# Two table scatters of a slot taken apart in GpSimd's order, in a fused perceiver kernel

## The reference, cut to what matters

```python
x = x + _L0_xattn_ref(_layernorm(x), ctx_1024, ...)
x = x + _L0_attn_ref(_layernorm(x), ...)
x = x + _L0_ffn_ref(_layernorm(x), w1, w2)          # quantised weights and activations
x = x + _L1_xattn_ref(_layernorm(x), ctx_1024, ...)  # 16 heads
x = x + _L1_attn_ref(_layernorm(x), ...)             # window of 5
x = x + _L1_ffn_ref(_layernorm(x), router_w, w1, w2)

# in _L1_ffn_ref
top_v, top_i = jax.lax.top_k(softmax(x_flat @ router_w.T), 2)
for k in range(2):
    pos = ...        # place of the row in its expert's list
    slot = jnp.where(pos < C, eid * C + pos, E * C)
    buf = zeros.at[slot].add(x_flat * keep)
    out = out + expert(buf)[slot] * gate * keep
```

## Time and profile before

| what | value |
| --- | --- |
| median of 3 runs | 1499.72 us (1499.08 to 2269.69) |
| profiled execution | 1499.72 us, span 1497.9 us |
| TensorE | busy 1395.7 us, 93% |
| weight loads | 1188.2 us, 79% |
| VectorE | 886.7 us, 59% |
| ScalarE | 826.6 us, 55% |
| GpSimd | 639.2 us, 43% |

### The profile page before, as it was taken

The page is one execution under the profiler, slowest core; times in us unless marked ns, Lnnn a source line. Parts: engine busy times, 40 slices in busy tenths (PEclk is TensorE's granted clock), DMA queues, the critical chain, the costliest instruction groups (busy, mean ns, idle before and its releaser), DMA issues. The chain is left out here.

```text
span 1497.9 us, 51669 instructions
## 1 busy us (share of the span) xinstructions
PE 1395.7 (93%) x19618; PEld 1188.2 (79%) x19619; DVE 886.7 (59%) x3115; ACT 826.6 (55%) x2392; POOL 639.2 (43%) x1194
## 2 busy tenths in 40 slices
PE   6789999999999999999999986199999999999997
PEld 4467778878877887887788765099999999999997
DVE  4668888899999999999999865111111111111111
ACT  0488888888888888888888871011111111111111
POOL 1233444444445455454545444534443443444443
PEclk7999999999999999999999996599999999999999
DMA  9323434334343433434333132256666666666653
GB/s 330 128 69 98 119 98 112 109 104 115 105 115 98 111 103 111 115 96 123 99 92 100 66 129 75 73 171 175 180 183 187 184 176 175 177 184 189 183 178 81
DMA packets 91024, 199.05 MB, mean 133 GB/s; under 512 B 13552, under 2 KB 48112, under 8 KB 79696
## 3 DMA queue, kind: packets, MB, share of 16 engines
q1 hardware_dynamic: 72160, 174.42, 37.1%
q0 software_dynamic: 15680, 18.69, 6.6%
q10 hardware_dynamic: 2992, 3.28, 0.6%
HBM read 178.32 MB, written 18.29 MB: 131 GB/s over the span
## 5 line engine op out<-in xcount | busy, mean ns | idle before, releaser
L1827 ACT ACTIVATE heT<-ps 128x512 f32<-128x512 f32 x142 | 84.8, 597 | 445.8 <-PE ps L1809 445.8
L1809 PEld LDWEIGHTS ps<-xeT,w_block 128*128 128x128 f32 x2272 | 267.6, 194 | 5.2 <-issue 0.9
L1809 PE MATMUL ps<-xeT,w_block 128*128 128x128 f32 x2272 | 268.2, 277 | 1.1 <-issue 0.6
L928 ACT ACTIVATE x_prob<-ps,x_nmax 128x257 f32<-128x257 f32 x512 | 237.3, 473 | 44.7 <-DVE x_nmax L1335 39.5
L1795 PE MATMUL ps<-contexts,heT 128*128 x1136 | 256.8, 379 | 0.0
L1795 PEld LDWEIGHTS ps<-contexts,heT 128*128 128x128 f32 x1136 | 210.4, 190 | 25.7
L1335 DVE TENSOR_REDUCE x_nmax<-ps 128x2 f32<-128x514 f32 x256 | 169.0, 681 | 21.3 <-PE ps L655 21.2
L663 PE MATMUL ps<-constants,x_prob 128*128 128x128 f32 x1024 | 152.2, 281 | 12.5 <-ACT x_prob L928 11.1
L1766 DVE COPY to_ix<-places 128x1 uint32 x71 | 10.9, 154 | 246.0 <-PE ps L1795 136.6
L1841 POOL TENSOR_TENSOR rt_hold<-constants 128x1 f32<-128x1 f32 x142 | 40.4, 284 | 262.8 <-DVE ye L1767 100.7
L932 ACT ACTIVATE x_probT<-ps 128x512 f32<-128x512 f32 x256 | 147.4, 632 | 3.6 <-PE ps L663 3.6
(11 more groups left out here) (275 smaller groups left out, 2918.1 us busy)
## 6 DMA issues: line engine op xcount, KB each, us to landing
w_block<-in_m_w SPq DMA_DIRECT2D x71, 1024.0 KB
contexts<-in_cT SPq DMA_DIRECT2D x112, 257.0 KB, 3.0
contexts<-in_cn SPq DMA_DIRECT2D x112, 256.0 KB, 4.0
contexts<-in_m_w SPq DMA_DIRECT2D x8, 1024.0 KB, 6.2
contexts<-in_cT SPq DMA_DIRECT2D x4, 1028.0 KB, 11.9
xin<-in_x SPq DMA_DIRECT2D x32, 128.0 KB, 2.4
lastq<-in_lastq SPq DMA_DIRECT2D x32, 128.0 KB, 2.6
contexts<-in_cn SPq DMA_DIRECT2D x4, 1024.0 KB, 12.8
```

What stands on the lines that cost most here:

```text
L928: A(p1[u % 2][:, r, :], ps[:, r, 0:KEYS], ACT.Exp, bias=nmax1[u % 2][:, r:r + 1], accum_out=rsum1[u % 2][:, r:r + 1]).then_inc(e1_ok.handl ...
L1809: t = mm(ps[:, 2 * b + n, f * P:(f + 1) * P], w1[b][:, k, lo:lo + P], xeT[b][:, k, :], start=k == 0, stop=k == H - 1)
L1827: A(heT[b][:, n * FK // 2:(n + 1) * FK // 2, :].rearrange("p k t -> p (k t)"), ps[:, 2 * b + n, :], ACT.Gelu).then_inc(heT_ok.handle, 1)
```

## The change

In GpSimd's slot the two scatters of a slot's tile stood side by side behind unit_select(1). The first (k = 0) moves one step ahead, before unit_select(1); the second (k = 1) moves behind the three rstd steps, in front of unit_last(2).

```diff
@@ -1131,12 +1131,12 @@
                 at(s + 5, c0_bias)
                 at(s + 2, unit_last, 1)
                 at(s + 1, s1_rstd)
+                scatter(s - 1, 0)
                 at(s + 2, unit_select, 1)
-                scatter(s - 1, 0)
-                scatter(s - 1, 1)
                 at(s + 3, q1_rstd)
                 at(s + 6, c0_rstd)
                 at(s + 4, ff_rstd)
+                scatter(s - 1, 1)
                 at(s + 2, unit_last, 2)
```

## The result

The changed kernel took 1510.32 us (median of 5 runs) and the kernel before 1500.38 us beside it: ratio 1.0059, 95% interval 1.0038 to 1.0080. The medians differ by 9.9 us, the ratio and its interval stand for 8.9 us (5.7 to 12.0): one run of each kernel was slow (2172.71 and 2269.69 us; the slow run of the changed kernel at a granted clock of 0.58) and counts in the medians alone. The forecast was 5.1 us slower, with a range up to 1509.0 us. So the sign was right and the size too small by nearly a factor of two. The profiled execution of the changed kernel is a long one, 1516.72 us (span 1514.9).

A forecast was written before the change was run, and what follows sets the result against it. TensorE, busy 93% of the span, was taken as the bound. 16 slots x 0.34 us = 5.4 us, less 0.3 us for the first scatter, gave 5.1 us on 1499.7: 1504.8 us, range 1499.2 to 1509.0.

The forecast's parts named there:

- TensorE as the bound: Tile loop: TensorE has 0.3 us to spare per slot, so its stall lengthens a slot by nearly its own length.
- The pair hidden where it stood: GpSimd before query_var_eps, which waits 0.86 us more for VectorE's moments; taking one scatter away there brings nothing.
- The first scatter's move: GpSimd, ahead of x_select: cost 0, and 0.2 us given back once at VectorE's self_prob; 0.3 us allowed in all.
- GpSimd's new times: Behind ffn_in_rstd: scatter of 1.05 us, then first query_blocks product 0.34 us later, some 2.2 instead of 1.88 us after ffn_in_rstd's start.
- Slots: 16: Tile loop: of the slots holding a pair, only 12 to 27 lose time from the second scatter's move.
- the release of ffn_rounded: VectorE: ffn_rounded held by the first query_blocks product until 673.43, taking 0.65 to 0.7 us instead of 0.35.
- The first half of the coupling: VectorE beside GpSimd: the later first query_blocks product starts at 673.01, 0.08 us ahead of ffn_rounded, and so holds it.
- The term: TensorE at L604: ffn_xq ends later, so TensorE stalls 0.34 us more in each of 16 slots, 5.4 us.
- the case of the whole lock: Upper bound for the unshown item, the second scatter in its new place: 0.65 us in each slot.
- Rival 1: VectorE's ffn_rounded goes before the first query_blocks product and stays at 0.35 us; no loss, 1499.4 us; chance 20%.
- Rival 2: The moved scatter itself holds VectorE's ffn_in_norm, to near 1 us; ffn_xq 0.7 us late, 1510.6 us; chance 11%.
- Rival 3: Stall appears at L604, but a later TensorE wait in the slot absorbs it; about 1500.5 us; chance 9%.

The follow-up runs named there:

- e1: Kernel before with only the first scatter moved, ahead of x_select 1; 1496.10 against 1499.35 us, ratio 0.9978.
- e2: Kernel before with only the second scatter moved, behind ffn_in_rstd; 1508.97 us, ratio 1.0076.
- e8: Changed kernel, with query_blocks also waiting until ffn_xq of the same slot is done; 1492.75 against the kernel before's 1501.02 us, ratio 0.9935.
- g1: Kernel before with the first scatter ahead of x_select 1 and query_blocks waiting for ffn_xq; 1491.20 against 1499.76 us, ratio 0.9952.
- h2: Kernel before with the second scatter directly ahead of query_blocks, no wait between, first scatter in its old place; 1534.92 against 1546.92 us, ratio 0.9918.
- e3: Kernel before with both scatters moved behind ffn_in_rstd; 1516.11 us, ratio 1.0124.
- f2: Extra 448-column GpSimd product behind ffn_in_rstd, first scatter before x_select 1, second behind query_blocks; 1510.13 us, ratio 1.0076 against the kernel before.
- f1: Changed kernel, with the first query_blocks product waiting by semaphore for x_select 0 to be complete; 1507.26 against the kernel before's 1499.76 us, ratio 1.0053.
- e4: Kernel before, scatters in their old place, with x_lastv of unit 2 waiting for x_rinv, so query_blocks comes later; 1508.27 us, ratio 1.0056.
- h1: Kernel before, scatters in their old place, with an extra 448-column GpSimd product directly ahead of query_blocks; 1564.42 against 1546.92 us, ratio 1.0103.
- g2: Kernel before with first scatter ahead of x_select 1, second behind query_blocks, and query_blocks waiting for ffn_xq; 1511.53 against 1499.76 us, ratio 1.0082.
- i1: The changed kernel repeated in the last session; 1518.01 against the kernel before's 1547.79 us, ratio 0.9811.
- i4: Repeat in the last session of the kernel before with the second scatter directly ahead of query_blocks; 1534.23 against 1547.79 us, ratio 0.9908.

## Why the prediction was right and wrong

- TensorE as the bound, and a stall of it lengthening a slot by its own length: right. L604 comes 0.58 to 0.68 us later and the slot is 0.60 us longer.
- The pair hidden where it stood: right for the first sessions (query_var_eps waits 2.37 us now). But the first of the pair stretched TensorE's L674 run in the same moment (1.02 us instead of 0.76), which the row 663.80 of TensorE's timeline showed and I did not read, and in the last sessions the pair cost far more that way.
- The first scatter's move: its sign was right, its size and its reason not. e1 gained 3.3 us, not 0.3. The prediction counted VectorE's self_prob alone; TensorE's L674 runs are 2.7 us shorter. Of this the slots of the one profiled execution show 1.5. In the changed kernel the gain can't be told apart: its slots are as long as those of e2 (26.86 and 26.85).
- GpSimd's new times: right to 0.01 us (2.23 against 2.22). Slots: 16, right. The expert stage holds no change of the order; the 4.8 us more behind the slots in the profiled execution go with its lower clock.
- The failed step is the release of ffn_rounded, "which is then held until 673.43", that is through the first product alone. The first half of the coupling, that the later products catch ffn_rounded, was right. I took from 855.62 that a step gets through 0.42 us after the first product's start. That row had a wait ahead of its products. Behind a scatter with no wait since, VectorE gets in only 0.46 us after the start of the second one: 1.10 to 1.20 us instead of 0.65 to 0.7, so L604 at 3.95 instead of 3.66. The term was 0.34 us a slot and measured 0.60: 16 x 0.60 = 9.6 us instead of 5.4, inside the measured 5.7 to 12.0. The prediction did name a bound of 0.65 us in each slot, "the case of the whole lock", but gave it no rival and no chance, and its own sum for it (16 x 0.65 less 0.3, 1509.8 us) lies above the range that it then stated.
- The scatter itself does hold VectorE a little: ffn_in_norm took 0.54 us instead of 0.41, and I had read from self_norm's 0.41 at 913.47 that it would not. e8 keeps the 0.54 and its L604 is 0.14 us later than in g1, though the two times can't be told apart. And where a step arrives at another moment the scatter holds it for longer: 0.52 us in h2, 0.43 us in some tiles of e3. The Trainium skill ("SBUF — State Buffer", section "Who interferes with whom") has the pair of ports held for a whole instruction. For the scatter the runs speak against that: ffn_in_norm began 0.26 us into a scatter of 1.05 us and lost 0.13 us, ffn_rounded of h2 began 0.28 us into one and lost 0.52, and x_own_half lost nothing. For query_blocks the trace agrees only roughly: a held step gets through 0.41 to 0.52 us after the start of a product that the timeline shows for 0.61 to 0.66 us. The same section counts a VectorE product with both inputs in SBUF among those that contend with GpSimd's reads; x_own_half is one, and its 0.81 us beside f2's product agree.
- Rival 1 (the race the other way) fell; the margin was 0.19 us and not 0.08 (680.24 and 680.43), as ffn_in_norm was 0.13 us late. Rival 2's time, 1510.6 us, is the nearest to the measured one, but by luck: ffn_in_norm grew to 0.54 us and not to near 1, so its mechanism gives 0.13 us. The step is held for a microsecond by what follows the scatter, not by the scatter. Rival 3 fell: nothing absorbed the stall.
- No rival had the circumstances of the last sessions, in which the change wins 30 us. The profile of before has no gap in its L674 stretches, but it has the mild form, 0.82 to 1.19 us instead of 0.76, and I had not looked at it.

## What to carry to other kernels

Read durations, not only waits: a step that takes 0.6 us in one tile and 0.3 in another is being held, and here the whole result went through such a step without any semaphore. Before a long instruction is moved on GpSimd's queue, look at which of its products then follow it without a wait and which VectorE steps arrive meanwhile; let the products wait for the step that TensorE needs, as in e8 and g1. Compare the same run of instructions with and without a DMA beside it, on TensorE too: 1.02 against 0.76 us was the sign of what came in the last sessions. And a DMA from GpSimd's queue beside such a dense stretch of short TensorE instructions is a risk of its own, so measure such a change in more than one session.

## What the runs showed that I had not expected

- Behind an indirect DMA of GpSimd, products that follow without a wait keep VectorE out until the last is well under way: 1.19 us in the changed kernel, 1.76 us in e3 (four products), 1.25 us in h2. It is not without exception: in tile 17 of e3 VectorE gets in behind x_lastv and again behind the first query_blocks product, and in the last tile of e8 and f1 ffn_rounded runs beside x_lastv unhurt. After a wait (e4, f1) or behind a long product (h1), VectorE gets in 0.41 to 0.52 us after the start of a query_blocks product. Why the DMA does this was not shown.
- TensorE's run of 64 short products (one every 12 ns, 0.76 us in all) is lengthened by a scatter beside it. In the first sessions a scatter that started between 0.2 us before and 0.3 us after the run's start made it 0.82 to 1.19 us, and one that started 0.64 to 0.85 us ahead left it at 0.76 (e1 and the changed kernel). In the last two it took about 3 us with the pair side by side (three gaps of about 0.5 us) and 1.1 to 1.3 us in the changed kernel. With the pair there the granted clock fell as well, and the slot was 2.8 us longer. Which circumstance brings the gaps on stays open; if equal numbers mean equal chips it is not the chip alone, as the session of f1 to g2 and that of i1 to i4 were both on the one numbered 6. Whether it is TensorE's instruction supply that the scatter holds up was not tested.
